# Graph network, one core: message aggregation in three fp32r terms with its operands' rests on GpSimd, and three moves in the engines' order

## The reference

```python
x = _layernorm(x + L0(x, adj))       # adj @ (x @ W) + bias
x = _layernorm(x + L1(x, adj))       # only the first 25 nodes
x = _layernorm(x + L2(x, adj))       # adjacency-weighted softmax, below: norm 2 with statistics(2)
# L3, with s = x @ w_se.T + b_se and dist the squared distances of s
A = jnp.exp(-dist) * mask                        # P in the kernel
msg = jax.nn.relu(x @ w_msg.T + b_msg)
x_nmp = jnp.einsum('bnm,bmd->bnd', A, msg)       # the message aggregation
x_in = jnp.concatenate([x_conv, x_nmp], axis=-1)
gi = x_in @ w_ih.T + b_ih;  gh = x @ w_hh.T + b_hh
r = sigmoid(gi_r + gh_r);  z = sigmoid(gi_z + gh_z)
nn_ = jnp.tanh(gi_n + r * gh_n)
x = _layernorm(x + (1.0 - z) * nn_ + z * x)
```

## Time and profile before

| | |
|---|---|
| median of 3 runs | 581.17 us (580.17 to 582.27) |
| the profiled execution: its own time | 581.22 us |
| its span | 579.3 us, granted clock 0.994 |
| busy TensorE, VectorE, ScalarE, GpSimd | 96%, 81%, 62%, 20% |
| one steady turn | 31.71 us |

### The profile page before, as it was taken

One profiled execution on the slowest core, in us unless ns is written; L12 is line 12 of the kernel. 1 busy time (PEld: TensorE's weight loads), 2 busy tenths in 40 slices (PEclk: granted clock), 3 DMA queues, 4 the chain that ended last, 5 costly groups with the idle time before them and its releaser, 6 DMA issues.

```text
span 579.3 us, 11740 instructions
## 1 busy us (share of the span) xinstructions
PE 556.5 (96%) x3583; PEld 476.0 (82%) x3583; DVE 466.5 (81%) x1768; ACT 359.2 (62%) x758; POOL 118.7 (20%) x143
## 2 busy tenths in 40 slices
PE   6788999999999999999999999999999999999994
PEld 5667897988889797979788897979797988889584
DVE  4888767988888887878888888878788888888665
ACT  2325565666676666766766767667667666776452
POOL 3411130213122130302131221303021312113010
PEclk9989999999999999999999999999999999999998
DMA  7890050030301103030303011030303030000000
GB/s 201 263 298 16 2 167 32 2 112 1 90 21 42 68 0 110 0 110 0 110 0 107 3 56 53 7 103 0 110 0 110 0 110 0 20 1 19 2 19 18
DMA packets 33300, 34.46 MB, mean 59 GB/s; under 512 B 1663, under 2 KB 22531, under 8 KB 33146
## 3 DMA queue, kind: packets, MB, share of 16 engines
q1 hardware_dynamic: 32986, 34.01, 18.3%
q10 hardware_dynamic: 288, 0.13, 0.1%
HBM read 29.74 MB, written 4.39 MB: 59 GB/s over the span
## 4 chain that ended last, share of the span: by engine, by line
PE 84%; DVE 1%; ACT 1%; issue 1%; POOLq 0%; POOL 0%; DVEq 0%; ACTq 0%
PE bank L260 14%; PE bank L262 13%; PE bank L261 13%; PE bank L1787 9%; PE pair L262 6%; PE pair L261 6%; PE pair L260 6%; PE bank L1619 4%; PE bank L1630 3%; PE bank L1723 2%; PE pair L1779 2%; PE pair L1711 2%; PE bank L1684 1%; PE bank L1729 1%; PE pair L1738 1%
## 5 line engine op out<-in xcount | busy, mean ns | idle before, releaser
L1148 POOL TENSOR_TENSOR rs<-ve,neg_half 128x4 f32<-128x4 f32 (+1 forms) x60 | 54.8, 914 | 278.1 <-DVE ve L1345 244.0
L260 PE MATMUL bank<-cd_hi,w_hi 128*128 128x256 f32 x272 | 77.1, 283 | 0.0
L261 PE MATMUL bank<-cd_lo,w_hi 128*128 128x256 f32 x272 | 76.5, 281 | 0.0
L262 PE MATMUL bank<-cd_hi,w_lo 128*128 128x256 f32 x272 | 76.2, 280 | 0.0
L1787 PE MATMUL bank<-P,msg 128*128 128x512 f32 x128 | 57.6, 592 | 0.0
L1377 DVE TENSOR_TENSOR P<-bank,aT 128x512 f32<-128x512 f32 x64 | 41.2, 686 | 18.3 <-ACT bank L1197 18.2
L261 PEld LDWEIGHTS bank<-cd_lo,w_hi 128*128 128x128 f32 x272 | 51.2, 188 | 1.6
L260 PEld LDWEIGHTS bank<-cd_hi,w_hi 128*128 128x128 f32 x272 | 51.3, 189 | 1.4
L260 PE MATMUL pair<-aT_hi,x_hi 128*128 128x512 f32 x128 | 51.3, 401 | 0.2 <-DVE aT_lo L560 0.2
L262 PEld LDWEIGHTS bank<-cd_hi,w_lo 128*128 128x128 f32 x272 | 51.5, 189 | 0.0
L262 PE MATMUL pair<-aT_hi,x_lo 128*128 128x512 f32 x128 | 50.4, 394 | 0.0
(11 more groups left out here) (368 smaller groups left out, 1527.6 us busy)
## 6 DMA issues: line engine op xcount, KB each, us to landing
adj_nat<-in_adj_dram SPq DMA_DIRECT2D x16, 1024.0 KB, 6.6
x_nat<-in_x_dram SPq DMA_DIRECT2D x16, 256.0 KB, 2.9
xt<-in_x_dram SPq DMA_DIRECT2D x3, 1280.0 KB, 11.6
out_dram<-y_out SPq DMA_DIRECT2D x15, 256.0 KB, 2.3
hw<-in_L_gnn_W_dram SPq DMA_DIRECT2D x2, 640.0 KB, 6.7
xt<-in_L_gnn_conv_w_dram SPq DMA_DIRECT2D x1, 1088.0 KB, 5.9
aT<-in_adj_dram SPq DMA_DIRECT2D x5, 96.0 KB
nat_ih<-in_L_gnn_w_ih_dram SPq DMA_DIRECT2D x1, 384.0 KB, 5.8
```

What stands on the lines that cost most here:

```text
L260: nc.tensor.matmul(o, lh, rh, start=start, stop=False)
L261: nc.tensor.matmul(o, lh, rl, start=False, stop=False)
L262: return nc.tensor.matmul(o, ll, rh, start=False, stop=stop)
L1148: g.tensor_tensor(rs[i][:, 0:n], ve[i][:, 0:n], neg_half[:, 0:n], ALU.pow).then_inc(po_rs[i], 1)
```

## The change

In turns with `cur` and `new` (0 to 13) the message aggregation is 12 fp32r matmuls: ScalarE makes `P_hi` of each chunk and `msg_hi`, GpSimd `P_lo`, VectorE `msg_lo`. Turns 14 and 15 keep the fp32 form. TensorE's order in these turns is new: transposes 0 and 1, the hidden-state parts of the z and r gates, transpose 2, the aggregation (first the 8 matmuls on `P_hi`, then the 4 on `P_lo`), the gate parts on xc, then those on nmp. On ScalarE the output stands behind exponentials 2 and 3 and three of the roundings, where it stood between exponentials 1 and 2. The new x's rest goes from VectorE to GpSimd, and its semaphore is now called `x_rest`. The statistics of norm 3 are finished before nmp_lo and the adjacency rests 0 and 1, and normalise stays behind those. In turn 15 the tanh of n stands behind co_hi on ScalarE, and co_lo in front of gu on VectorE. The tiles `msg_hi`, `msg_lo` (128x512), `P_hi` and `P_lo` (128x4x512) are new. Left out below are their declarations, the semaphores' names and the renamings.

```diff
@@ -1175,8 +1180,18 @@
                                         ).then_inc(po_rs[3], 1)
+                if cur and new:
+                    for mc in range(NC):
+                        wait(pool, ac_Phi[mc], V(1))
+                        wait(pool, pe_N, V(0))
+                        g.tensor_tensor(P_lo[:, mc, :], P[:, mc, :], f(P_hi[:, mc, :]), ALU.subtract).then_inc(po_Plo[mc], 1)
                 if nxt:
                     inverse_root(V, 2, 2)
+                if new:
+                    wait(pool, ac_xhi, V(3))
+                    wait(pool, x_in[par], dma(2))
+                    wait(pool, pe_agg2, V(2))
+                    g.tensor_tensor(x_lo[:, :, :], x_nat[par][:, :, :], f(x_hi[:, :, :]), ALU.subtract).then_inc(x_rest, 1)
             over_graphs(pool, turn)
@@ -1195,6 +1210,20 @@
                     s.activation(AT_BANK[mc % 2][:, :], AT_BANK[mc % 2][:, :], ACT.Exp, scale=2.0).then_inc(ac_E[mc], 1)
+
+                def output():
+                    wait(act, po_shift, V(0))
+                    wait(act, o_out, outs)
+                    wait(act, dv_less, V(0))
+                    for c in range(NC):
+                        last = s.activation(y_out[:, c, :], X_BANK[:, ch(c)], ACT.Identity, bias=shift[:, c:c + 1],
+                                            scale=rs[3][:, c:c + 1])
+                    last.then_inc(ac_out, 1)
+
+                def round_weighed(mc):
+                    wait(act, dv_P[mc], V(1))
+                    wait(act, pe_N, V(0))
+                    s.activation(P_hi[:, mc, :], P[:, mc, :], ACT.Identity).then_inc(ac_Phi[mc], 1)
@@ -1212,9 +1241,12 @@
                                      ).then_inc(ac_nn, 1)
-                elif prev:
+                def tanh_n():
                     wait(act, dv_t, V(0))
                     s.activation(SQ_BANK[:, :], gh, ACT.Tanh, bias=cols[:, BIH + 2:BIH + 3]).then_inc(ac_nn, 1)
+
+                if prev and nxt:
+                    tanh_n()
                 if cur:
@@ -1231,6 +1263,8 @@
                     s.activation(co_hi[:, :], c1[:, 1, 0:TW], ACT.Identity).then_inc(ac_coh, 1)
+                if prev and cur and not nxt:
+                    tanh_n()
                 if cur:
@@ -1239,7 +1273,10 @@
                     wait(act, dv_s, V(1))
-                    wait(act, pe_N, V(0))
+                    if new:
+                        wait(act, dv_msglo, V(0))
+                    else:
+                        act.wait_ge(pe_N, V(0))
                     s.activation(msg_v[1], ms_half(ms_banks(nxt)[1]), ACT.Relu).then_inc(ac_msx, 1)
@@ -1256,6 +1293,10 @@
                     s.activation(LR[0:KD, 1, :], SQ_BANK[GR:GR + KD, :], ACT.Identity).then_inc(ac_LR, 1)
+                if cur and new:
+                    wait(act, ac_msg, V(1))
+                    wait(act, pe_N, V(0))
+                    s.activation(msg_hi[:, :], msg[:, :], ACT.Identity).then_inc(ac_msghi, 1)
                 if nxt:
@@ -1271,14 +1312,10 @@
                     exponential(1)
-                if prev and cur:
-                    wait(act, po_shift, V(0))
-                    wait(act, o_out, outs)
-                    wait(act, dv_less, V(0))
-                    for c in range(NC):
-                        last = s.activation(y_out[:, c, :], X_BANK[:, ch(c)], ACT.Identity, bias=shift[:, c:c + 1],
-                                            scale=rs[3][:, c:c + 1])
-                    last.then_inc(ac_out, 1)
+                if cur and new:
+                    round_weighed(0)
+                elif cur:
+                    output()
                 if nxt:
@@ -1289,6 +1326,13 @@
                     exponential(3)
+                if cur and new:
+                    round_weighed(1)
+                    round_weighed(2)
+                    round_weighed(3)
+                    if prev:
+                        output()
+                if cur:
                     wait(act, dv_conv, V(1))
@@ -1373,7 +1417,10 @@
                     wait(dve, ac_E[mc], V(1))
-                    wait(dve, pe_N, V(0))
+                    if new:
+                        wait(dve, po_Plo[mc], V(0))
+                    else:
+                        dve.wait_ge(pe_N, V(0))
                     v.tensor_tensor(P[:, mc, :], AT_BANK[mc % 2][:, :], aT[par][:, mc, :], ALU.mult
@@ -1464,10 +1511,10 @@
                 if prev:
+                    if not nxt:
+                        rest_of_odd()
                     wait(dve, ac_nn, V(0))
                     v.tensor_tensor(gu, x3T[1 - par][:, :], SQ_BANK[:, :], ALU.subtract).then_inc(dv_u, 1)
-                    if not nxt:
-                        rest_of_odd()
                     wait(dve, dv_u, V(0))
@@ -1570,6 +1617,10 @@
                     v.tensor_tensor(odd, HN_BANK[:, 0:HALF], base[:, 1, :], ALU.add).then_inc(dv_conv, 1)
+                if cur and new:
+                    wait(dve, ac_msghi, V(1))
+                    wait(dve, pe_N, V(0))
+                    v.tensor_tensor(msg_lo[:, :], msg[:, :], f(msg_hi[:, :]), ALU.subtract).then_inc(dv_msglo, 1)
                 if nxt:
@@ -1592,18 +1643,13 @@
                     hold(dve, dv_y3, V(2))
-                    statistics(2, V, 2, lambda c: y3[:, c, :], EPS, rests_meanwhile)
-                else:
+                    statistics(2, V, 2, lambda c: y3[:, c, :], EPS, None if new else rests_meanwhile)
+                if new or not nxt:
                     rests_meanwhile()
...
                 if new:
-                    wait(dve, ac_xhi, V(3))
-                    wait(dve, x_in[par], dma(2))
-                    wait(dve, pe_agg2, V(2))
-                    v.tensor_tensor(x_lo[:, :, :], x_nat[par][:, :, :], f(x_hi[:, :, :]),
-                                    ALU.subtract).then_inc(dv_xlo, 1)
                     split_rest(2)
@@ -1778,29 +1824,58 @@
                     last.then_inc(pe_out2, 1)
-                if cur:
-                    wait(pe, ac_msg, V(1))
-                    if prev:
-                        wait(pe, ac_out, V(0))
-                    for mc in range(NC):
-                        wait(pe, dv_P[mc], V(1))
-                        last = t_.matmul(X_BANK[:, :], msg[:, ch(mc)], P[:, mc, :], start=(mc == 0), stop=(mc == NC - 1))
-                    last.then_inc(pe_N, 1)
+                def gate_part(o, blk, hi, lo, start, stop):
+                    return three(pe, o, w_hi[:, blk, :], w_lo[:, blk, :], hi[:, :], lo[:, :], start, stop)
+
                 if new:
...
                         transpose_adjacency(mc)
+                if cur and not new:
+                    pe.wait_ge(ac_msg, V(1))
+                    pe.wait_ge(ac_out, V(0))
+                    for mc in range(NC):
+                        pe.wait_ge(dv_P[mc], V(1))
+                        last = t_.matmul(X_BANK[:, :], msg[:, ch(mc)], P[:, mc, :], start=(mc == 0), stop=(mc == NC - 1))
+                    last.then_inc(pe_N, 1)
+                if cur and nxt and not new:
+                    pe.wait_ge(dv_xclo, V(1))
+                    gate(MS_BANK[:, :], of_state(1) + of_inputs(1), pe_z, 1)
+                    gate(CV_BANK[:, :], of_state(0) + of_inputs(0), pe_r, 1)
+                if cur and new:
+                    wait(pe, ac_msg, V(1))
+                    gate_part(MS_BANK[:, :], HH + 1, x3T_hi, x3T_lo, True, False)
+                    wait(pe, dv_conv, V(1))
+                    gate_part(CV_BANK[:, :], HH, x3T_hi, x3T_lo, True, False)
+                if new:
                     wait(pe, dv_conv, V(1))
                     transpose_adjacency(2)
-                if cur and nxt:
+                if cur and new:
+                    if prev:
+                        wait(pe, ac_out, V(0))
+                    wait(pe, dv_msglo, V(1))
+                    for mc in range(NC):
+                        wait(pe, ac_Phi[mc], V(1))
+                        t_.matmul(X_BANK[:, :], msg_hi[:, ch(mc)], P_hi[:, mc, :], start=(mc == 0), stop=False)
+                        t_.matmul(X_BANK[:, :], msg_lo[:, ch(mc)], P_hi[:, mc, :], start=False, stop=False)
+                    for mc in range(NC):
+                        wait(pe, po_Plo[mc], V(1))
+                        last = t_.matmul(X_BANK[:, :], msg_hi[:, ch(mc)], P_lo[:, mc, :], start=False, stop=(mc == NC - 1))
+                    last.then_inc(pe_N, 1)
+                if cur and new:
                     wait(pe, dv_xclo, V(1))
-                    gate(MS_BANK[:, :], of_state(1) + of_inputs(1), pe_z, 1)
-                if cur and nxt:
-                    gate(CV_BANK[:, :], of_state(0) + of_inputs(0), pe_r, 1)
+                    gate_part(MS_BANK[:, :], IH + 2, xc_hi, xc_lo, False, False)
+                    gate_part(CV_BANK[:, :], IH, xc_hi, xc_lo, False, False)
                 if cur and new:
                     wait(pe, dv_y3, V(2))
-                    gate(SQ_BANK[:, :], of_inputs(2), pe_gn, 1)
```

(26 more changed lines are left out.)

## The result

The changed kernel takes 576.11 us in the median of 4 runs (575.17 to 576.64), the kernel before 581.22 beside it. The ratio is 0.9897 with a 95% interval of 0.986 to 0.9934: some 1% faster, about 5.1 us. The forecast was 576.2.

A forecast was written before the change was run, and what follows sets the result against it. TensorE was taken to bound the steady turns. Per turn 0.66 - 0.25 - 0.10 = 0.31 us, times 14 = 4.3, plus 0.7 for the last tanh: 581.2 - 4.3 - 0.7 = 576.2 us, range 573.0 to 580.5.

The forecast's parts named there:

- TensorE bounds the turn: Thirteen turns of 31.7 us have no idle TensorE time, so a matmul removed shortens the turn unless a wait returns it.
- The form, 0.66 us: Message aggregation: 12 fp32r matmuls take 2.77 us instead of 3.43, saving 0.66 us per turn, 9.2 us in 14.
- The stall at the transposes, 0.25: TensorE at transposes 0 and 1: new wait for VectorE's P of chunk 3, 0.25 us per turn.
- The stall at x3, 0.10: TensorE before the x3 transposes: wait for norm 3's normalise, now behind the adjacency rests, about 0.1 us per turn.
- The turn: Steady turn 31.4 us: 0.66 - 0.25 - 0.10 = 0.31 us saved per turn, 4.3 us over 14.
- the tanh: Turn 15, tanh behind co_hi: TensorE's last taps start earlier, saving 0.7 us, bounds 0 and 0.9.
- the sum: Whole kernel: 581.2 - 4.3 - 0.7 = 576.2 us.
- Output, P_hi, P_lo, msg_lo at nothing: Moved output and new roundings before the message matmuls cost nothing; output is ready 0.2 us before it is wanted.
- Contention, taken as nothing with 1.1 us of idle time to hold it: GpSimd holding off VectorE's two-SBUF-input operations: VectorE's 1.1 us idle before nmp_lo just holds it, no cost.
- the bound: Contention: VectorE's msg_lo, dq and xc_lo each wait for a P_lo; bounds no cost and 0.5 us per turn.
- The second rival: GpSimd and VectorE hold each other off, nmp_lo 0.5 us late, then rests and x3; time 583.3 us; chance 0.10.

The follow-up runs named there:

- e9: Changed kernel with only the 12 fp32r message matmuls in turns 0 to 13 replaced by the 4 fp32 matmuls: turn 31.99, time 584.59 us.
- e3: Changed kernel with GpSimd making P_lo only in turn 0, later turns reusing it: turn 31.37, time 575.24 us.
- e5: Changed kernel with the new x's rest back on VectorE, behind normalise and ahead of chunk 2's adjacency rest: turn 31.98, time 585.17 us.
- e2: As e1, with the output on ScalarE also moved back between exponentials 1 and 2: turn 31.15, time 572.54 us.
- e4: Changed kernel with norm 3's aggregate, variance and power back behind nmp_lo and two adjacency rests: turn 34.08, time 614.14 us.
- e1: Changed kernel with the z gate's hidden-state part moved ahead of transposes 0 and 1 on TensorE: turn 31.28, time 575.02 us.
- e8: As e2, with msg_lo on VectorE moved ahead of weighing chunk 0: turn 31.16, time 572.93 us.
- e10: Changed kernel with msg_lo made twice on VectorE in turns 0 to 13, first into a spare tile: turn 32.73, time 595.45 us.
- e11: As e4, with GpSimd's x rest ahead of norm 3's power instead of behind it: turn 33.20, time 600.94 us.

## Why the prediction was right, point by point

- **TensorE bounds the turn**: right. 0.62 us put back into its work (e9) came out in full, while 1.3 us taken from VectorE (e3) changed nothing. It holds for VectorE's work in front of nmp_lo; behind normalise VectorE has no room, and 0.61 us more there lengthened the turn by 0.61 (e5).
- **The form, 0.66 us**: 0.62 by e9, and 2.88 against 3.43 in the timelines with 0.09 of record. Right within 0.04.
- **The stall at the transposes, 0.25**: 0.22 in the timeline, 0.22 by e2. Of the delay from VectorE to TensorE I counted 0.15, the row had 0.13, and the timeline after has at most 0.12 at the x3 transposes (259.48 + 1.11 to 260.71); e4 has 0.06 there (273.53 + 1.97 to 275.56).
- **The stall at x3, 0.10**: wrong in place. Shifted by the 0.73 us between the two turns' starts, nmp_hi, the second rest and normalise were forecast for 256.28, 258.87 and 259.48, and that is where they are. The extra 0.03 of latency and of rounding at either end made a wait out of what is a tie: x3 is seen at 260.71, when transpose 3 is through. A stall of 0.05 stands at the fourth chunk of the x aggregation, where I had said that there is neither stall nor room.
- **The turn**: 31.37 where 31.40 was forecast; 14 x 0.34 = 4.8 us where 4.3 was. With the tanh's 0.69 (forecast 0.7) this is 5.5. In the profiled execution the spans differ by 4.5 only, since its first part, which the change doesn't touch, was 0.99 us longer (x3 of turn 0 at 72.83 against 71.84). Of this 0.60 stand at the first adjacency's transposes, which wait for its transfer (11.61 against 11.01); for the other 0.39 no cause is shown, but the granted clock from 40 to 55 was 0.89, where the kernel before had 1.00. The medians differ by 5.1. That the sum came within 0.1 us of the median is luck to some 0.5 us.
- **Output, P_hi, P_lo, msg_lo at nothing**: right, with little room: 0.2 us were forecast for the output, 0.09 were there, and e1 shows it as the next wait.
- **Contention, taken as nothing with 1.1 us of idle time to hold it**: the result is right. VectorE's operations were held off as the bound had it (msg_lo 1.37, dq 0.78), 1.3 us together; nmp_lo came 0.09 late (257.00, and not 0.63 behind 256.28) and had 0.4 of room, and e3 shows that the idle time took the rest. But the working missed a hold: GpSimd is held off too (P_lo of chunk 2 1.73 beside msg_lo, 1.29 in e8). So dq ended at 253.69, where the working, shifted by the 0.73, has 253.17, and the variance at 257.06 and not 256.77.
- **The second rival** had the right mechanism, in both directions, and its times hold as far as dq (253.82 by it, 253.69 measured). Two things kept it from coming true. Its last hold is missing: xc_lo ran in 0.68 us, and the variance ended 0.36 before the rival's time. And the rival let nmp_lo's delay of 0.5 pass on to x3, while the two adjacency rests behind nmp_lo wait for ScalarE anyway (0.20 and 0.29 idle at 257.89 and 258.87), which would have taken most of it; this is worked out from the rows, no run tests it. That the changed kernel stands near an edge is shown by e10, where one more operation of the kind makes it slower than the kernel before. There msg_lo, and not nmp_lo, meets TensorE first.
- **What was given no price of its own**: I took the reordering of norm 3 and the x rest's move as conditions of the sum. They are worth 2.7 and 0.6 us per turn in the changed kernel (e4, e5), together more than the form; of the 2.7, 0.88 are the hold between normalise and the x rest (e11). With the form but without one of them the turn is longer than before the change (34.08 and 31.98 against 31.71), and all the rest without the form is a loss of 0.28 (e9).

## What to carry to other kernels

When the bounding engine is full, first write its new list with the old durations, and then only the chains that end at its waits. That gave the turn to 0.03 us here, and every experiment to 0.1 except two: in e4 a hold by GpSimd was left out (0.88), and in e10 the largest wait, for msg_lo, was not among those followed (0.4). A start that is taken from a record has to be counted from its neighbours' pace, as e1 shows. A move that takes cover away from a wait (here the fp32 matmuls in front of the transposes) costs what it covered; look for a piece with no such input to put in its place, as the z gate's hidden part, and then for what is late next (here ScalarE's output). Price the operations of GpSimd by what they do to VectorE's, not by their own length.

## What the runs showed of the hardware that was not expected

A VectorE operation with only one tensor input in SBUF, normalise (128x128 to 128x128, two scalars per partition), is held off by GpSimd as well: four of them took 1.97 us beside GpSimd's x rest and 1.11 without (e4, e11). In e10, where it began at 266.94 and the x rest ended at 267.44, the four took 1.35. I had only counted operations with two SBUF inputs. The Trainium skill, GPSIMD Engine Reference (Key points), names both: instructions in a 2-port mode and such with two SBUF inputs. The runs show the hold, not the mode.

xc_lo (two SBUF inputs, SBUF output) kept its 0.68 us in the changed kernel, starting at 254.84 when the last P_lo, which ends at 254.94, was all but through. What counts is the overlap in time, which a list of operations alone doesn't show.

The hold goes both ways: P_lo took 1.29 us alone and 1.73 beside msg_lo, and in e8, where xc_lo starts first (250.86), the P_lo that starts at 250.89 took 1.81.
